# Linear attention on one NeuronCore: the state matmuls in high and low parts, the keys' parts made on GpSimd, gathered rows in a ring of sixteen

## The reference, cut to what matters

```python
qkv = x @ W
q, k, v = jnp.split(qkv, 3, axis=-1)
q = jax.nn.elu(q) + 1.0
k = jax.nn.elu(k) + 1.0
KV = jnp.einsum('bld,blh->bhd', k, v)
k_sum = k.sum(axis=1)
Z = 1.0 / (jnp.einsum('bld,bd->bl', q, k_sum) + EPS)
V = jnp.einsum('bld,bhd,bl->blh', q, KV, Z)
x = _layernorm(x + V, axis=-1)
```

## Time and profile before

| | |
|---|---|
| three runs, median (lowest to highest) | 1495.3 us (1493.47 to 1497.02) |
| the profiled execution's own time | 1496.07 us |
| its span in the profile | 1494.3 us |
| PE busy / weight loads | 92% / 81% |
| DVE, ACT, POOL busy | 59%, 41%, 46% |
| granted TensorE clock, mean | 0.962 of full speed |

### The profile page before, as it was taken

The page is one execution under the profiler, slowest core; times in us unless marked ns, Lnnn a source line. Parts: engine busy times, 40 slices in busy tenths (PEclk is TensorE's granted clock), DMA queues, the critical chain, the costliest instruction groups (busy, mean ns, idle before and its releaser), DMA issues. The chain is left out here.

```text
span 1494.3 us, 27884 instructions
## 1 busy us (share of the span) xinstructions
PE 1378.0 (92%) x8959; PEld 1203.4 (81%) x8960; DVE 877.4 (59%) x1763; ACT 612.8 (41%) x1077; POOL 683.3 (46%) x556
## 2 busy tenths in 40 slices
PE   7996599899999993899879999999999997999997
PEld 3454488788888883777669999999999977999997
DVE  5788422222222223577578787887887853666655
ACT  4554323233333331766543332332333324555553
POOL 6663287777660004340026665665655644350500
PEclk9998699999999996999979999999999998999999
DMA  4102325222310004310032264464463577465450
GB/s 166 60 28 94 119 81 149 95 98 101 124 70 14 14 15 134 120 57 1 1 127 85 85 183 123 142 170 110 146 193 96 157 222 270 154 214 184 147 201 31
DMA packets 109194, 171.17 MB, mean 115 GB/s; under 512 B 6128, under 2 KB 95088, under 8 KB 101712
## 3 DMA queue, kind: packets, MB, share of 16 engines
q1 hardware_dynamic: 100112, 156.00, 32.2%
q0 software_dynamic: 3408, 9.31, 2.2%
q10 hardware_dynamic: 5616, 5.11, 1.0%
HBM read 114.96 MB, written 55.44 MB: 114 GB/s over the span
## 5 line engine op out<-in xcount | busy, mean ns | idle before, releaser
L1636 PE MATMUL disp_psS<-disp_e,last_x 128*128 128x256 f32 x1024 | 233.1, 381 | 4.0 <-POOL disp_e L1723 4.0
L1636 PEld LDWEIGHTS disp_psS<-disp_e,last_x 128*128 128x128 f32 x1024 | 191.2, 191 | 28.6 <-POOL disp_e L1723 4.6
L1621 PE MATMUL disp_psL<-phi_hold,hand_xh 128*128 (+1 forms) x1024 | 199.8, 296 | 4.6 <-DVE disp_e L1788 4.4
L1730 POOL TENSOR_TENSOR disp_s<-disp_e 128x512 f32<-128x512 f32 x64 | 82.3, 1286 | 264.4 <-ACT disp_e L1706 264.4
L1909 PE MATMUL comb_psO<-phi_hold,comb_eh 128*128 (+1 forms) x1024 | 197.6, 290 | 0.4 <-DVE comb_el L2007 0.3
L1621 PEld LDWEIGHTS disp_psL<-phi_hold,hand_xh 128*128 128x128 f32 x1024 | 165.1, 193 | 8.5 <-issue 5.5
L1688 ACT ACTIVATE disp_raw<-disp_psL 128x512 f32<-128x512 f32 x128 | 76.4, 597 | 222.3 <-PE disp_psL L1621 157.8
L1909 PEld LDWEIGHTS comb_psO<-phi_hold,comb_eh 128*128 128x128 f32 x1024 | 156.3, 189 | 1.0 <-DVE comb_el L2007 0.9
L1723 POOL TENSOR_TENSOR disp_e<-disp_e,disp_rs 128x1024 f32<-128x1024 f32 x64 | 151.5, 2368 | 0.0
L1621 PE MATMUL disp_psL<-phi_hold 128*128 (+1 forms) x512 | 145.7, 285 | 0.0
L1909 PE MATMUL comb_psO<-phi_hold,comb_el 128*128 (+1 forms) x512 | 143.7, 281 | 0.0
(11 more groups left out here) (259 smaller groups left out, 3112.1 us busy)
## 6 DMA issues: line engine op xcount, KB each, us to landing
logits<-disp_raw SPq DMA_DIRECT2D x64, 512.0 KB, 4.1
hand_e<-logits SPq DMA_DIRECT2D x32, 1024.0 KB, 6.6
w_raw<-in_w SPq DMA_DIRECT2D x8, 2048.0 KB, 7.9
disp_wt<-in_w_slot SPq DMA_DIRECT2D x16, 1024.0 KB, 7.9
w_raw<-in_w SPq DMA_DIRECT2D x8, 1024.0 KB, 10.4
disp_bt<-in_b_slot SPq DMA_DIRECT2D x8, 1024.0 KB, 11.3
slot_y<-disp_yb SPq DMA_DIRECT2D x60, 128.0 KB, 3.2
comb_y_in<-slot_y SPq DMA_DIRECT2D x3, 2048.0 KB, 10.5
```

What stands on the lines that cost most here:

```text
L1621: last = nc.tensor.matmul(psL[p][:, b, :], xp[:, kd, t * P:(t + 1) * P], pp[:, kd, bass.ds(k * BLK, BLK)], start=b % 2 == 0 and kd == 0 an ...
L1636: last = nc.tensor.matmul(psS[kd][:, b, :], x[:, b * TB + mc, kd * P:(kd + 1) * P], e[mc % 4][:, b, :], start=mc == 0 and b % 2 == 0, stop ...
L1730: nc.gpsimd.tensor_tensor(s2[:], e[mc % 4][:, 0:2, :], e[mc % 4][:, 2:4, :], ALU.add).then_inc(pair_sum, 1)
```

## The change

In the routing stage, semaphores are merged: the one-hot and the difference raise one semaphore `picked`, the last matmul raises `counted`, and the token table raises `tables_ready`; each wait stands where it stood.

In the linear attention:

- `yg`, the gathered rows, becomes a ring of sixteen tiles instead of thirty-two; a gather into it waits for the same projection as before.
- ACT copies the values to `vh` in fp32r instead of `v1`. DVE gets a new step `values`, behind `keys` of the same tile: `vl`, the projection in PSUM less `vh`. PE's projection of tile t waits for `v_low` to reach t - 1, that is for `values` of the tile two back.
- POOL gets `split_keys`, two instructions per tile of 128x256: `kh` is `kk` plus a zero (fp32r), and `kl` is `kk` less `kh`, behind a wait on its own `kh`. It stands behind the tile's gather in passes 0 and 1, and alone in passes 2 and 3.
- `add_up` makes three fp32r matmuls of 258 columns in place of one f32 matmul of 257, for each of the two chunks (kh by vh, kl by vh, kh by vl), and waits for `k_split` and `v_low`. The 258th column is zero.
- The columns behind the values are filled at the stage's start by copies from a small tile.

The diff of `linear_attention`, cut to the changed lines:

```diff
@@ -1096,7 +1096,7 @@
...
     with ctx:
-        yg = m.sb("yg", [P, NT, D])
+        yg = m.sb("yg", [P, 2 * TB, D])
         xh = m.sb("xh", [P, KD, TB, P], F32R)
@@ -1110,7 +1110,13 @@
...
         kk = [m.sb(f"kk{i}", [P, D]) for i in range(KB)]
-        v1 = [m.sb(f"v1{i}", [P, D + 1]) for i in range(KB)]
+        kh = [m.sb(f"kh{i}", [P, D], F32R) for i in range(KB)]
+        kl = [m.sb(f"kl{i}", [P, D], F32R) for i in range(KB)]
+        VW = D + 2
+        vh = [m.sb(f"vh{i}", [P, VW], F32R) for i in range(KB)]
+        vl = [m.sb(f"vl{i}", [P, VW], F32R) for i in range(KB)]
+        tail = m.sb("tail", [P, 4])
+        zero = m.sb("zero", [P, 1])
         kv = m.sb("kv", [P, KD, D + 1])
@@ -1163,7 +1170,7 @@
...
                 wait(pool, k_raw, t - 2 * TB + 1)
-                nc.gpsimd.indirect_dma_start(yg[:, t, :], None, ys_dram,
+                nc.gpsimd.indirect_dma_start(yg[:, t % (2 * TB), :], None, ys_dram,
                                              bass.IndirectOffsetOnAxis(route["place"][:, t:t + 1], 0)).then_inc(gathered[t if t < TB else TB - 1 + t // TB], 16)
@@ -1173,13 +1180,23 @@
...
 
+            def split_keys(t):
+                pool.wait_ge(k_ready, t + 1)
+                nc.gpsimd.tensor_tensor(kh[t % KB][:], kk[t % KB][:], zero[:].to_broadcast([P, D]), ALU.add).then_inc(k_split, 1)
+                pool.wait_ge(k_split, 2 * t + 1)
+                nc.gpsimd.tensor_tensor(kl[t % KB][:], kk[t % KB][:], kh[t % KB][:].bitcast(F32), ALU.subtract).then_inc(k_split, 1)
+
             for t in range(2 * TB):
                 fetch(t)
-            for b in range(2, B):
-                for t in range(b * TB, (b + 1) * TB):
-                    fetch(t)
-                for i in range((b - 2) * TB, (b - 1) * TB):
-                    low_part(i)
+            pool.wait_ge(ones_set, 2 + 2 * KB)
+            for b in range(B):
+                for j in range(TB):
+                    if b < B - 2:
+                        fetch((b + 2) * TB + j)
+                    split_keys(b * TB + j)
+                if b < B - 2:
+                    for i in range(b * TB, (b + 1) * TB):
+                        low_part(i)
 
@@ -1208,11 +1225,12 @@
...
                     t = s * TB + j
-                    wait(pe, k_ready, t + 1)
-                    wait(pe, kv_read, 3 * (t + 1))
+                    wait(pe, k_split, 2 * t + 2)
+                    wait(pe, v_low, t + 1)
                     for chunk in range(KD):
-                        last = nc.tensor.matmul(psC[chunk][:, 0:D + 1], kk[t % KB][:, chunk * P:(chunk + 1) * P], v1[t % KB][:],
-                                                start=j == 0, stop=j == TB - 1)
+                        for a, (kp, vp) in enumerate(((kh, vh), (kl, vh), (kh, vl))):
+                            last = nc.tensor.matmul(psC[chunk][:, 0:VW], kp[t % KB][:, chunk * P:(chunk + 1) * P], vp[t % KB][:],
+                                                    start=j == 0 and a == 0, stop=j == TB - 1 and a == 2)
                     last.then_inc(added, 1)
@@ -1220,6 +1238,7 @@
...
                     wait(pe, kv_read, 3 * (t - 1))
+                    wait(pe, v_low, t - 1)
                     for k in range(KD):
@@ -1287,7 +1306,7 @@
...
                 wait(act, added, t - KB + 1)
-                a_.activation(v1[t % KB][:, 0:D], psK[j % 2][:, D:2 * D], ACT.Copy).then_inc(kv_read, 1)
+                a_.activation(vh[t % KB][:, 0:D], psK[j % 2][:, D:2 * D], ACT.Copy).then_inc(kv_read, 1)
 
@@ -1356,7 +1375,7 @@
...
                 wait(dve, normed, s * TB)
-                v.scalar_tensor_tensor(xb[:, j, :], yg[:, t, :], route["prob"][:, t:t + 1], x[:, t, :], ALU.mult, ALU.add).then_inc(summed, 1)
+                v.scalar_tensor_tensor(xb[:, j, :], yg[:, t % (2 * TB), :], route["prob"][:, t:t + 1], x[:, t, :], ALU.mult, ALU.add).then_inc(summed, 1)
                 if j > 0:
@@ -1384,6 +1403,11 @@
...
 
+            def values(s, j):
+                t = s * TB + j
+                wait(dve, kv_read, 3 * t + 3)
+                v.tensor_tensor(vl[t % KB][:, 0:D], psK[j % 2][:, D:2 * D], vh[t % KB][:, 0:D].bitcast(F32), ALU.subtract).then_inc(v_low, 1)
+
             def keys(s, j):
@@ -1414,7 +1438,13 @@
...
             for i in range(KB):
-                v.memset(v1[i][:, D:D + 1], 1.0).then_inc(ones_set, 1)
+                if i == 0:
+                    v.memset(zero[:], 0.0).then_inc(ones_set, 1)
+                    v.memset(tail[:, 1:4], 0.0)
+                    v.memset(tail[:, 0:1], 1.0).then_inc(ones_set, 1)
+                    dve.wait_ge(ones_set, 2)
+                v.tensor_copy(vh[i][:, D:VW], tail[:, 0:2]).then_inc(ones_set, 1)
+                v.tensor_copy(vl[i][:, D:VW], tail[:, 2:4]).then_inc(ones_set, 1)
             dve.wait_ge(wh_ready, 1)
@@ -1423,6 +1453,7 @@
...
                         keys(s - 1, j)
+                        values(s - 1, j)
                         if j % 2 == 1:
```

More of the change, by code:

```diff
@@ L613, in normalise_and_route @@
         psI = m.ps("psI", [P, 2 * NCOL])
-        (w_loaded, chain, kept, turned, xT_ready, scored, scores_ready, routed, diff_ready, exp_ready,
-         onehot_ready, counted, tables_ready, tabled, token_ready, stored) = (m.sem(s) for s in (
-             "w_loaded", "chain", "kept", "turned", "xT_ready", "scored", "scores_ready", "routed", "diff_ready",
-             "exp_ready", "onehot_ready", "counted", "tables_ready", "tabled", "token_ready", "stored"))
+        (w_loaded, chain, kept, turned, xT_ready, scored, scores_ready, routed, exp_ready,
+         picked, counted, tables_ready, stored) = (m.sem(s) for s in (
+             "w_loaded", "chain", "kept", "turned", "xT_ready", "scored", "scores_ready", "routed",
+             "exp_ready", "picked", "counted", "tables_ready", "stored"))
         filled = m.sem("filled")
@@ L646, in _ @@
             pool.wait_ge(stored, 16 * B)
-            pool.wait_ge(token_ready, 1)
+            pool.wait_ge(tables_ready, 5)
             for slot in range(FIRST_GATHERS):
@@ L686, in _ @@
             pe.wait_ge(filled, 4)
-            pe.wait_ge(onehot_ready, 1)
+            pe.wait_ge(picked, 1)
             flat = lambda ap: ap.rearrange("p t e -> p (t e)")
@@ L699, in _ @@
                 last = nc.tensor.matmul(psI[:], rows1[:, t // TG, :, t % TG], ids[:, t // TG, :, t % TG], start=t == 0, stop=t == NT - 1)
-            last.then_inc(tabled, 1)
+            last.then_inc(counted, 1)
         @block.scalar
@@ L717, in _ @@
             out(NT // GT - 1)
-            act.wait_ge(diff_ready, 1)
+            act.wait_ge(picked, 2)
             nc.scalar.activation(expd[:], expd[:], ACT.Exp).then_inc(exp_ready, 1)
@@ L749, in _ @@
             link(v.tensor_reduce(bidx[:], cand[:], X, ALU.min))
[L750 to L751 removed]
+            v.tensor_tensor(onehot[:], bc(bidx[:]), over_t(c["eidx"][:]), ALU.is_equal).then_inc(picked, 1)
+            v.tensor_tensor(expd[:], logit[:], bc(best[:]), ALU.subtract).then_inc(picked, 1)
             dve.wait_ge(counted, 1)
@@ L1131, in linear_attention @@
          stat_in, stat_out, root_in_ready, root_out_ready, normed, finished, chain) = (m.sem(s) for s in names)
+        v_low, k_split = m.sem("v_low"), m.sem("k_split")
         phi_loaded, phi_high = m.sem("phi_loaded"), m.sem("phi_high")
@@ L1301, in _ @@
             a_.activation(wh[:], w_raw[:], ACT.Copy).then_inc(wh_ready, 1)
-            act.wait_ge(ones_set, KB)
+            act.wait_ge(ones_set, 2 + 2 * KB)
             for j in range(TB):
```

6 lines of the change are left out of this document (2 added, 4 removed).

## The result

Changed kernel: 1519.5 us median (1519.15 to 1520.26, 4 runs); before: 1494.4 (1492.98 to 1497.02, 4 runs). Ratio 1.0163, 95% interval [1.015, 1.0175]: slower by 24 us (22 to 26). The forecast was 1516, in a range from 1501 to 1522. The profiled execution took 1520.26 us (span 1518.3).

The account below looks back on a forecast made before the run. PE was taken to bound the pass. Order and queue, less PE's saving, gave +7.1 us, and with contention +20.7: 1496.07 + 20.7 = 1516.8, beside the median 1516; range 1501 to 1522.

Parts of the forecast that it names:

- PE's saving: State sum on PE: six fp32r matmuls, 0.71 us for 0.86; saves 0.15 us a tile, 4.9 in all.
- values behind the chains: PE waits for `values` behind `root_out` and `root_in`: 2.0 us at projection 3, 1.0 at projection 7; 0.9 in pass 3.
- rival 3: All passes: neither contention nor a POOL queue, only PE's waits for `values`; +3.4 us, 1498.7; chance 0.06.
- Contention: DVE steps with both inputs in SBUF are held until POOL's running instruction ends; lifts the sum from +7.1 to +20.7 us.
- the replay: Pass 1 followed step by step, DVE and POOL waiting for each other: +8.2 us; all four passes +20.7.
- Rival 1: DVE and POOL don't hold each other noticeably on 256-column steps, only order and queue count; +7.1 us, 1502.4; chance 0.19.
- The tail on POOL: End of pass 1: after keys 5, three pairs and two gathers in series before PE's last sum; 6.6 + 0.5 us.
- The output halves are not touched: Output halves after the passes: claimed to stay as they were, difference 0, only moving with what precedes them.
- rival 2: As forecast, plus TensorE's clock falling in PE's pauses, three or four times; some +5 us, 1521; chance 0.10.

Follow-up runs that it names:

- e1: Changed kernel with the low parts of keys and values left out: PE's new sum alone, no new DVE or POOL step; 1493.33 us, ratio 0.9989.
- e2: e1 with the `values` step on DVE and PE's waits for it, still no GpSimd pairs; 1502.77 us, ratio 1.0047.
- e3: e2 with the GpSimd pairs back in place and size, but on tiles that nobody reads; 1516.88 us, ratio 1.013.
- e11: e3 with the unread GpSimd pairs at 128x64 instead of 128x256; 1501.77 us, ratio 1.0038.
- e9: Changed kernel in full, but ACT writes the keys' high part and GpSimd only the low part; 1511.76 us, ratio 1.0108.
- e10: Changed kernel in full, but the keys' high part is on ACT and their low part on DVE, none on GpSimd; 1513.42 us, ratio 1.0117.

## Why the prediction was right

Its direction, its size (1516 against 1519.5) and its passes hold, in part by luck, as the last points say. By its steps:

- **PE's saving**, 0.15 us a tile: measured 0.14. But I counted all of it (4.9 us), and e1, which has nothing else, got 1.6 (interval 0.3 to 3.0). I had taken it that every us off PE's list shows in the end, and had not asked what ends a pass next. It is DVE's list up to `root_in`, with ACT's `norm_in` and copy of the state behind it. I had both engines at eight tenths, which is a mean: DVE is without a gap until `root_in` is done.
- **values behind the chains**, without contention: I had 2.0 us at projection 3 of pass 1 and e2 shows 1.98; 1.0 at projection 7 and 0.57; 0.9 in pass 3 and 0.86. The long waits were right; their sum with the saving, +3.4 (rival 3's working), came out at +7.0. The profiled stage has +5.2: pass 2 with its clock is 1.0 us over my figure and the other passes 0.7 together. The rest lies outside the stage and is not explained.
- **Contention**, 20.7 - 7.1 = 13.6 us: e3 less e2 is 12.4 (8.6 to 16.2), falls of the clock included, which I had not put in. In the changed kernel keys 1 of pass 1 begin at 652.12, where the replay has them at 647.4 less 0.76, plus the 5.6 us by which pass 1 starts later: 652.2. The pause at projection 3 was 2.65 against 2.8, the one at projection 7 2.66. Rival 1, no hold, is refuted.
- **The tail on POOL**: after keys 5, three pairs and two gathers, forecast at 6.6 + 0.5 us. They ran from 667.30 to 674.87, 7.6 us:

```profile
667.30 0.61 POOL L1185 TENSOR_TENSOR lin_kh<-lin_kk,lin_zero 128x256 fp32r<-128x256 f32 x1 [2.41 <-DVE lin_kk L1415]
...
671.96 1.47 POOL L1173 DMA_INDIRECT lin_yg<-sorted_y,table_place  x1
...
674.15 0.72 POOL L1187 TENSOR_TENSOR lin_kl<-lin_kk,lin_kh 128x256 fp32r<-128x256 f32 x1
```

- **"The output halves are not touched"** is the sentence that failed. One of the four took 2.2 us more, behind the pauses of 2.07 and 0.75 us, at a granted clock of 0.77. That is the mechanism of rival 2, in a place where I had not put it, and it is most of the 3.5 us by which the forecast fell short. I had held it unlikely because PE "waited often and shortly" at full clock before; the changed kernel's pauses are longer.
- **Luck.** The four passes together came out at +20.9 against +20.7, though the clock fell in two of them, which is not in the forecast. Where one pass can be set beside another with and without such a fall, it costs 0.8 us (passes 2 and 1 of e2) and 1.05 (pass 1 of e11, which has the narrow ghosts too, and of e2). So, as an estimate from these two, the replay was too long elsewhere by 1.5 to 2 us. The saving lost in e1 is not one of these terms: in the changed kernel PE waits 0.75 us for the copy in every pass, as before.

Left open: what decides whether the clock falls behind a pause. Of the changed kernel's four pauses of 2.65 us inside the passes, two were followed by a fall and two were not. The comparison of e9 and e10 with the rest rests on different lots.

## What to carry to other kernels

Where one engine fills a stage, cheaper work for it pays only as far as the next engine's queue allows, so ask first what ends the stage then; here more than half of the saving was gone before the costs began (of 4.9 us, 1.6 were left by the ratio and 2.2 in the profiled stage). A mean busy share hides this: look for the stretch in which the next engine has no gap, and for who waits on its end. Work put on an engine "with room" has to be costed by what it does to its neighbour's steps and to the queue that the full engine waits on: the same GpSimd pairs cost 4 us in a kernel where PE hardly waited for DVE and 12 in one where it did. And a pause of PE can cost twice, once itself and once in the clock behind it; if it can't be removed, filling it may pay.
